# A perceiver layer with a mixture of experts: the router's work moved from behind the attention rounds into them

## The reference, cut to what matters

```
x = x + cross_attention(ctx, layernorm(x))
x = x + linear_attention(layernorm(x))     # 16 heads of 64, elu + 1, causal over 32 tokens, sigmoid gate
xt = layernorm(x)                          # the router and the experts work on this
scores = xt @ gate_w.T                     # 8 experts
top_vals, top_idx = top_k(scores, 2)
top_w = softmax(top_vals)
h = silu(xt @ w1[e].T) * (xt @ w3[e].T)    # 1024 wide
x = x + sum over the two chosen e of top_w * (h @ w2[e].T)
```

## Time and profile before

| | us |
|---|---|
| median of 3 runs | 910.84 (908.56 to 913.74) |
| the profiled execution's own time | 905.29 |
| its span | 903.4 |
| TensorE busy | 811.7 (90%) |
| VectorE busy | 632.5 (70%) |
| ScalarE busy | 540.0 (60%) |
| GpSimd busy | 231.6 (26%) |
| first gather of the expert stage starts at | 508.21 |

### The profile page before, as it was taken

One profiled execution on the slowest core, in us unless ns is written; L12 is line 12 of the kernel. 1 busy time (PEld: TensorE's weight loads), 2 busy tenths in 40 slices (PEclk: granted clock), 3 DMA queues, 4 the chain that ended last, 5 costly groups with the idle time before them and its releaser, 6 DMA issues.

```text
span 903.4 us, 24127 instructions
## 1 busy us (share of the span) xinstructions
PE 811.7 (90%) x9192; PEld 704.3 (78%) x9192; DVE 632.5 (70%) x973; ACT 540.0 (60%) x846; POOL 231.6 (26%) x133
## 2 busy tenths in 40 slices
PE   3889869999999999998582699999999999999994
PEld 2555539889999899896582579888898898888984
DVE  3234332647567475563648399999999999999992
ACT  2433326726445365352131188898999989999881
POOL 1344410000000000000000024554555545555541
PEclk9899999999999999998655599999999999999997
DMA  9799970000000000006372125454554554545542
GB/s 351 274 391 387 382 298 1 3 4 1 3 2 3 4 3 3 3 3 274 112 269 93 58 91 142 122 153 131 139 149 120 153 136 131 152 124 149 142 117 58
DMA packets 34663, 115.84 MB, mean 128 GB/s; under 512 B 4290, under 2 KB 15491, under 8 KB 29475
## 3 DMA queue, kind: packets, MB, share of 16 engines
q1 hardware_dynamic: 27010, 104.35, 33.3%
q0 software_dynamic: 7584, 10.49, 6.5%
HBM read 105.26 MB, written 9.57 MB: 127 GB/s over the span
## 4 chain that ended last, share of the span: by engine, by line
PE 82%; DMA 7%; DVE 6%; issue 2%; ACT 1%; SPq 1%; POOLq 0%; DVEq 0%; ACTq 0%
PE ps L428 21%; PE ps L429 20%; PE ps L430 20%; DMA ctx_t<-in_ctxT 4%; PE ps L734 3%; PE ps L614 3%; PE ps L593 2%; PE ps L602 2%; PE ps L686 2%; PE ps L507 1%; PE ps L671 1%; PE ps L485 1%; PE ps L664 1%; PE ps L697 1%; PE ps L504 1%
## 5 line engine op out<-in xcount | busy, mean ns | idle before, releaser
L403 POOL DMA_INDIRECT xs_sb<-xn_d,slot_row x39 | 68.4, 1753 | 461.6 <-DVE slot_row L1315 384.7
L1195 DVE TENSOR_TENSOR w_lo<-w,w_hi 128x1024 fp32r<-128x1024 f32 x156 | 185.3, 1207 | 0.4 <-issue 0.4
L910 ACT ACTIVATE w_hi<-w 128x1024 fp32r x156 | 161.4, 1064 | 8.4 <-DVE tile_e L1276 7.3
L414 POOL DMA_INDIRECT out_x<-y_sb,slot_row x39 | 120.2, 3082 | 123.0 <-ACT y_sb L942 123.0
L428 PE MATMUL ps<-w_hi,xh 128*128 128x512 f32 x312 | 127.2, 408 | 1.3 <-DVE xl L1338 1.3
L430 PE MATMUL ps<-w_hi,xl 128*128 128x512 f32 x312 | 122.9, 394 | 0.0
L429 PE MATMUL ps<-w_lo,xh 128*128 128x512 f32 x312 | 122.9, 394 | 0.0
L428 PE MATMUL ps<-xT_hi,wa_hi 128*128 128x256 f32 x384 | 112.6, 293 | 1.5 <-DVE xT_lo L1089 1.5
L429 PE MATMUL ps<-xT_lo,wa_hi 128*128 128x256 f32 x384 | 108.9, 284 | 0.0
L430 PE MATMUL ps<-xT_hi,wa_lo 128*128 128x256 f32 x384 | 108.7, 283 | 0.0
L921 ACT ACTIVATE w_hi<-w_sb 128x1024 fp32r<-128x1024 f32 x78 | 82.8, 1062 | 34.1 <-DMA w_sb<-in_w 29.7
(11 more groups left out here) (180 smaller groups left out, 1690.3 us busy)
## 6 DMA issues: line engine op xcount, KB each, us to landing
w_sb<-in_w SPq DMA_DIRECT2D x78, 512.0 KB, 4.7
ctx_t<-in_ctxT SPq DMA_DIRECT2D x16, 1028.0 KB, 7.6
ctx_n<-in_ctxN SPq DMA_DIRECT2D x16, 1024.0 KB
w<-in_w SPq DMA_DIRECT2D x8, 2048.0 KB, 12.0
stage<-in_w_a SPq DMA_DIRECT2D x16, 256.0 KB, 5.4
x_all<-in_x SPq DMA_DIRECT2D x4, 512.0 KB, 7.4
out_x<-x_all SPq DMA_DIRECT2D x1, 2048.0 KB, 13.8
xn_d<-xn SPq DMA_DIRECT2D x4, 512.0 KB, 4.4
```

What stands on the lines that cost most here:

```text
L403: pool.indirect_dma_start(xs_sb[:, :], None, xn_d, bass.IndirectOffsetOnAxis(slot_row[:, t:t + 1], 0)).then_inc(f_xs, 16)
L414: pool.indirect_dma_start(out, bass.IndirectOffsetOnAxis(slot_row[:, t:t + 1], 0), y_sb[:, :], None, compute_op=ALU.add).then_inc(f_st, 16)
L910: act.activation(w_hi[:, c, :].rearrange("p (c n) -> p c n", c=DC), w13[:, bass.ds(e, 1), c % 2, :, c // 2 * 512:(c // 2 + 1) * 512].rearr ...
L1195: dve.tensor_tensor(w_lo[:, c, :].rearrange("p (c n) -> p c n", c=DC), w13[:, bass.ds(e, 1), c % 2, :, c // 2 * 512:(c // 2 + 1) * 512].re ...
```

## The change

The router's work for two tiles is done in the attention rounds, two rounds later: astep(r) does it for round r-2, and the last part for round r-3. There are eleven steps now, astep(0) to astep(10), in place of nine.

Each step has: the row statistics of round r-1 behind x2 (g_stats); the root on ScalarE behind den (g_sqrt), and the row scales on VectorE (g_rstd); the two normed tiles on ScalarE (g_lns); four transposes (g_trs) behind the sixth projection; their eviction (g_xT_ev); four logits products (g_logits) behind the second gate; their copy (g_scores); the two largest and their indices, one-hot choices and running counts (g_top) between the two gated halves; the exponential on ScalarE (g_exp), the weights (g_weights); two rank products (g_ranks) behind the first output projection; the place of each token inside its expert (g_places) with eight comparisons over 128 columns; and twelve scalings on ScalarE (g_whats). In the next step four products of 384 columns (g_table) add the round's tokens to a table by virtual tile, of which each expert has 16, and g_accept adds it up in SBUF. At the end, when all rounds are in, VectorE makes the experts' totals, offsets and a 0/1 selection matrix, and three products take the 39 used tiles out of the 128 virtual ones.

The numerators have three new waits, the second projection one. norm_att is cut in two, the first half placed earlier. The buffers gol and goT lie where expert 0's weights go, so that experts 0, 2 and 3 are loaded when the last projection is done, and only expert 1 early. POOL writes the output's residual and the normed tiles, two transfers a round. The four low splits of the first expert tile on VectorE stand in pairs behind the slot rows and behind the first x_lo.

```
+        load_expert(1)
         sp.wait_ge(a_v, 4 * NT // 2)
         for e in range(E // 2, E):
             load_expert(e)
         sp.wait_ge(a_num, NT)
         sp.wait_ge(a_y, NT // 2)
-        for e in range(EARLY + 1, E // 2):
+        for e in (0, 2, 3):
             load_expert(e)
-
-        sp.wait_ge(a_x2, NT // 2)
...
+        for r in range(NT // 2):
+            rows = slice(2 * r * P, (2 * r + 2) * P)
+            pool.wait_ge(a_x2, r + 1)
+            pool.dma_start(out[rows, :].rearrange("(t p) d -> p t d", p=P), x_all[:, 2 * r:2 * r + 2, :]).then_inc(o_init, 16)
+            pool.wait_ge(g_ln, 2 * r + 2)
+            pool.dma_start(xn_d[rows, :].rearrange("(t p) d -> p t d", p=P), xn3[:, r % 2, :, :]).then_inc(g_keep[r % 2], 16)
...
+                if n == 1:
+                    wait(pe, g_rk, 2 * (r - 2))
...
+            wait(pe, g_xT, r)
+            wait(pe, g_sc, r)
+            wait(pe, g_acc, r - 1)
...
+        def g_trs(r, u):
+            if not valid(r, NR):
+                return
+            wait(pe, g_ln, 2 * r + 2)
+            for dc in range(DC):
+                for s in range(2):
+                    m = pe.transpose(ps[:, 6, dc * 2 * P + s * P:dc * 2 * P + (s + 1) * P],
+                                     xn3[:, u, s, dc * P:(dc + 1) * P], ident)
+            m.then_inc(g_tr, 1)
+        def g_logits(r):
...
+            wait(pe, g_xT, r + 1)
+            wait(pe, a_de, min(2 * r + 4, NT))
+            for s in range(2):
+                for dc in range(DC):
+                    m = pe.matmul(ps[:, 5, s * E:(s + 1) * E], xT3[:, dc, s * P:(s + 1) * P], gw[:, dc, :],
+                                  start=dc == 0, stop=dc == DC - 1)
+            m.then_inc(g_mm, 1)
+        def g_ranks(r):
...
+            wait(pe, g_both, r + 1)
+            wait(pe, a_vu, min(4 * r + 12, 2 * NT))
+            pe.matmul(ps[:, 1, 0:2 * E], con[:, C_LOW:C_LOW + P], both[:, :, :].rearrange("p t e -> p (t e)"), start=True, stop=False)
+            pe.matmul(ps[:, 1, 0:2 * E], ones, count[:, 2 * r:2 * r + 2, :].rearrange("p t e -> p (t e)"),
+                      start=False, stop=True).then_inc(g_rank, 1)
+        def g_table(r):
...
+            wait(pe, g_what, r + 1)
+            wait(pe, a_de, min(2 * r + 6, NT))
+            for n in range(2 * TOP):
+                m = pe.matmul(ps[:, 4, 0:3 * P], in_tile[:, n, :], what[:, n, :, :].rearrange("p k s -> p (k s)"),
+                              start=n == 0, stop=n == 2 * TOP - 1)
+            m.then_inc(g_tab, 1)
             if now:
-                a_qks(r, range(2, 8))
-                a_gates(r)
+                a_qks(r, range(2, 6))
+            g_trs(r - 2, u)
+            if now:
+                a_qks(r, range(6, 8))
+                a_gates(r, range(0, 2))
+            g_logits(r - 2)
+            g_table(r - 3)
+            if now:
+                a_gates(r, range(2, 4))
             for s in range(2):
                 if before:
...
+                if s == 0:
+                    g_ranks(r - 2)
...
+        wait(pe, g_both, NR)
+        pe.matmul(ps[:, 3, 0:E], ones, count[:, NT, :], start=True, stop=True).then_inc(r_sum, 1)
+        pe.wait_ge(g_acc, NR)
+        pe.wait_ge(r_sel, 1)
+        pe.matmul(ps[:, 2, 0:SLOT_TILES], table[:, 0, :], sel[:, :], start=True, stop=True)
+        pe.matmul(ps[:, 2, SLOT_TILES:2 * SLOT_TILES], table[:, 1, :], sel[:, :], start=True, stop=False)
+        pe.matmul(ps[:, 2, SLOT_TILES:2 * SLOT_TILES], table[:, 2, :], sel[:, :], start=False, stop=True).then_inc(r_tab, 1)
...
+        def g_sqrt(r):
...
+            wait(act, g_var, r + 1)
+            act.activation(rstd3[:, :], rstd3[:, :], ACT.Sqrt, bias=eps[:, 0:1]).then_inc(g_sq, 1)
+        def g_lns(r, u):
...
+            wait(act, g_rs, 2 * r + 2)
+            wait(act, g_keep[u], 16 * (r // 2))
+            for s in range(2):
+                act.activation(xn3[:, u, s, :], x_all[:, 2 * r + s, :], ACT.Identity, scale=rstd3[:, s:s + 1],
+                               bias=shift3[:, s:s + 1]).then_inc(g_ln, 1)
+        def g_whats(r):
...
+            wait(act, g_pos, 8 * r + 8)
+            wait(act, g_w, r + 1)
+            wait(act, g_tab, r)
+            for n in range(2 * TOP):
+                t = 2 * r + n // TOP
+                for k, factor in enumerate((con[:, C_ID1 + t:C_ID1 + t + 1], w_h[:, n:n + 1].bitcast(F32), w_l[:, n:n + 1].bitcast(F32))):
+                    m = act.activation(what[:, n, k, :], in_slot[:, n, :], ACT.Identity, scale=factor)
+            m.then_inc(g_what, 1)
+            g_sqrt(r - 2)
             if now:
-                elu_parts(r, range(2, 8))
+                elu_parts(r, range(2, 4))
+            g_lns(r - 2, u)
+            if now:
+                elu_parts(r, range(4, 8))
+            g_xT_ev(r - 2)
+            if now:
                 for n in range(4):
...
+            g_exp(r - 2)
+            g_whats(r - 2)
...
+        def g_rstd(r):
...
+            wait(dve, g_sq, r + 1)
+            dve.reciprocal(rstd3[:, :], rstd3[:, :]).then_inc(g_rs, 1)
+            wait(dve, g_rs, 2 * r + 1)
+            dve.scalar_tensor_tensor(shift3[:, :], mean3[:, :], -0.5, rstd3[:, :], ALU.mult, ALU.mult).then_inc(g_rs, 1)
...
+        def g_top(r):
...
+            wait(dve, g_sc, r + 1)
+            for s in range(2):
+                dve.max(m8[:, s, :], sc[:, s, :]).then_inc(g_max, 1)
+            wait(dve, g_max, 2 * r + 2)
+            for s in range(2):
+                dve.max_index(i8[:, s, :], m8[:, s, :], sc[:, s, :]).then_inc(g_idx, 1)
...
+        def g_places(r):
...
+            wait(dve, g_what, r)
+            for n in range(2 * TOP):
+                dve.tensor_scalar(in_slot[:, n, :], con[:, C_I128:C_I128 + P], inf[:, n:n + 1], None, ALU.is_equal).then_inc(g_pos, 1)
+            wait(dve, g_pp, 7 * r + 7)
+            wait(dve, g_tab, r)
+            for n in range(2 * TOP):
+                dve.tensor_scalar(in_tile[:, n, :], con[:, C_I128:C_I128 + P], vtile[:, n:n + 1], None, ALU.is_equal).then_inc(g_pos, 1)
+            g_rstd(r - 2)
             recip(r - 1, 1)
+            if before:
+                norm_att(r - 1, 0)
...
-                norm_att(r - 1)
+                norm_att(r - 1, 1)
+            g_accept(r - 3)
+            g_scores(r - 2)
             a_lns(r + 1)
             if before:
-                for s in range(2):
-                    gated(r - 1, 1 - u, s)
-                    gated_lo(r - 1, 1 - u, s)
+                gated(r - 1, 1 - u, 0)
+                gated_lo(r - 1, 1 - u, 0)
+            g_top(r - 2)
+            if before:
+                gated(r - 1, 1 - u, 1)
+                gated_lo(r - 1, 1 - u, 1)
             a_lo_ev(r + 1)
             if r == 0:
                 w_out_lows()
+            g_weights(r - 2)
+            g_places(r - 2)
             if before:
                 x2(r - 1)
-                wait(dve, a_x2, r)
-                for s in range(2):
-                    stats_of(2 * (r - 1) + s, 2, a_bn)
-
+                g_stats(r - 1)
+
...
+        dve.wait_ge(r_sum, 1)
...
+        link(dve.reduce_sum(first[:, :], own[:, :, :], AX.X))
...
+        dve.tensor_scalar(sel[:, :], con[:, C_TILE:C_TILE + SLOT_TILES], goal[:, :], real[:, :], ALU.is_equal, ALU.mult).then_inc(r_sel, 1)
-        up_lo(0, range(4), expert(0))
...
+        up_lo(0, range(2), expert(0))
...
         x_lo(0)
+        up_lo(0, range(2, 4), expert(0))
```

More of the change, by code:

```diff
@@ L205, in build @@
-    assert at["late"] <= LATE_AT + EXP_BYTES
-    xT3 = place("xT3", [P, 2, DC, P])
-    IN_SLOTS = 4
-    sc = place("sc", [P, NT, E])
-    m8 = place("m8", [P, NT, 8])
-    i8 = place("i8", [P, NT, 8], U32)
-    i8f = place("i8f", [P, NT, 8])
-    first = place("first", [P, NT, E])
-    second = place("second", [P, NT, E])
-    both = place("both", [P, NT, E])
-    scan = [place(f"scan{i}", [P, NT + 8, E]) for i in range(2)]
-    cmp = place("cmp", [P, E, MAXT])
-    tiles = [place(f"tiles{i}", [P, 4 + E]) for i in range(2)]
@@ new lines, in build @@
+    dif3 = place("dif3", [P, 2])
+    sum3 = place("sum3", [P, 2])
+    sq3 = place("sq3", [P, 2])
+    rstd3 = place("rstd3", [P, 2])
+    shift3 = place("shift3", [P, 2])
+    sc = place("sc", [P, 2, E])
+    m8 = place("m8", [P, 2, 8])
+    i8 = place("i8", [P, 2, 8], U32)
+    pick = place("pick", [P, 2, TOP])
+    chosen = place("chosen", [P, 2 * TOP, E])
+    both = place("both", [P, 2, E])
+    count = place("count", [P, NT + 1, E])
+    dv = place("dv", [P, 2])
+    e1 = place("e1", [P, 2])
@@ new lines, in build @@
+    in_tile = place("in_tile", [P, 2 * TOP, P], F32R)
+    in_slot = place("in_slot", [P, 2 * TOP, P])
+    what = place("what", [P, 2 * TOP, 3, P], F32R)
+    table = place("table", [P, 3, P])
+    tiles = [place(f"tiles{i}", [P, 4 + E]) for i in range(2)]
+    assert at["low"] <= W13_AT, (at, W13_AT)
+    at["low"] = final_at
+    cmp = place("cmp", [P, E, MAXT])
+    own = place("own", [P, 2, E])
+    first = place("first", [P, 2])
```

(40 more changed lines are left out.)

301 lines of the change are left out of this document (153 added, 148 removed).

## The result

The changed kernel takes 917.97 us in the median of its runs (913.03 to 922.06); the kernel before took 908.56 beside it. The ratio is 1.010 with a 95% interval of 1.0061 to 1.0139, so it is slower by 1.0%. I had forecast 912.8 with a range of 901 to 923: the time lies in the range, and in the "slower" case rather than in the likeliest one.

A forecast was written before the change was run, and what follows sets the result against it. TensorE was taken to bound the attention rounds and an unoverlapped chain the tail. Span 903.4 + 23.7 (rounds) - 21.7 (tail) = 905.4 us, so a median of 912.8; likeliest 908 to 915, range 901 to 923.

The forecast's parts named there:

- "slower" case: Whole kernel: slower than before by more than 0.5% (4.6 us can't be told from no change); chance 0.35.
- What bounds the kernel: TensorE fills attention rounds, so work added there counts in full; nothing overlaps in the 84.3 us from last mask to gather.
- The wait: TensorE, at the transposes after the sixth projection, waits 1.9 us a round for ScalarE's normed tiles, behind two table loads.
- Rival 3: Attention rounds: TensorE isn't stalled at the transposes, giving back 11.4 us, 901.4; chance 0.25, shared with half of it plus short tail.
- rival 2: ScalarE: a table switch costs twice its load, in six steps and before the tail's roots; 18 us more, 931; chance 0.04.
- Added to each round: TensorE in attention rounds: router transposes 0.44, logits 0.65, ranks 0.33, table 0.70; together 2.1 us.
- Rounds: Six attention rounds: 5 x (2.1 + 1.9) + 1 x (1.4 + 1.9) = 23.3 us longer; a round 40.3 instead of 36.3.
- rival 1: Attention rounds: each stall drops TensorE's clock; six falls cost 10 us, 923; chance 0.18, counting falls in most rounds.
- Tail: Last mask to first gather of the expert stage: 62.6 us instead of 84.3, 21.7 saved; bounds 58 and 68.
- The sum: Whole kernel's span: 903.4 + 23.7 - 21.7 = 905.4 us; the median comes to 912.8.
- "no change": Whole kernel: median of 908 to 915 us, a difference under 0.5% (4.6 us); chance 0.40.
- Rival 4: Rounds and tail: more waits, VectorE late for masks or instruction fetches; 1 us a round, 2 in the tail, 921; chance 0.13.

The follow-up runs named there:

- a_logits2: Changed kernel with each round's logits computed twice (eight more products of 8 columns a round): 926.8 us, 1.0209 of the kernel before.
- b_pad: Kernel before with nine unused columns of constants, which move every buffer behind them by 32 bytes: 912.64 us, 1.0044 of the kernel before.
- b_xT32: Kernel before with only xT_hi and the buffers placed behind it moved by 32 bytes: 910.44 us, 1.0018 of the kernel before.
- a_pad24: Changed kernel with 24 more unused constant columns, putting xT_hi at 32 of 128 bytes: 915.07 us, 1.0071 of the kernel before.
- the fastest kernel: Changed kernel with the reciprocal root on VectorE and 24 more unused constant columns: 901.64 us, 0.9928 of the kernel before.
- a_trs_late: Changed kernel with the router's four transposes behind the eighth projection instead of the sixth: 921.68 us, 1.0129 of the kernel before.

## Why the prediction was right or wrong

**What bounds the kernel.** Right for the kernel before, and the mechanism held: work put into a round lengthens it (a_logits2: 0.83 us for 0.81), and work taken from the tail shortens the kernel. But the two don't cancel: the rounds gained 27 to 29 us and the tail lost 19. In the changed kernel the round is bound by TensorE and by a wait for ScalarE together.

**Work added to a round: 2.1 forecast, 2.5 measured, from the start of each group to the start of what follows.** Transposes 0.41 (0.44 forecast), logits 0.81 (0.65), table 0.80 (0.70), ranks 0.45 (0.33). I had taken the lowest of the bounds for the logits, by halving a row at half clock; the upper end was right.

**The wait: 1.9 forecast, 1.2 measured, at the forecast place and for the forecast reason.** It is read best in a round without a standstill of another kind behind its first projection, which starts at 248.55:

```profile
248.55 0.39 PE L443 MATMUL ps<-xT_hi,wa_hi 128*128 128x256 f32 x1
...
259.23 1.08 ACT L920 ACTIVATE xn<-x_all,shift,rstd 128x256 f32<-128x256 f32 x2
...
260.36 0.66 PE L656 MATMUL ps<-con,xn 128*128 128x128 f32 x4 [1.21 <-ACT xn L920]
```

The normed tiles are there at +11.8, 0.3 us before the forecast +12.1, since neighbouring instructions on ScalarE overlap (neg 0.20 behind the root's start). And TensorE comes to the transposes at +10.6, 0.4 later than the forecast +10.2, mostly because its products are slower (at +10.4 with 24 more constants). So part of the short wait is luck. Rival 3, no stall, is excluded, and so is rival 2, a switch at twice the load.

**A term that I didn't have: placement.** "Added to each round" counted instructions only. But the nine constants also moved the operands, and the 192 products of 256 columns a round started 0.120 instead of 0.117 us apart: 0.5 us a round. It is shown that the placement does this (b_pad, b_xT32) and costs 0.44% in the kernel before; in the changed kernel 0.1 of it hides behind the wait and 0.4 shows (a_pad24).

**Rounds: +23.3 forecast for six, +29.2 in the first profile, +27.2 in the second.** A full round was to be 4.0 us longer, 40.3. Less standstills the fifth is 4.5 longer, 40.77 against 36.29: 2.5 of work, 1.2 of wait and 0.5 of slower products are 4.2, and 0.3 stays open. The missed terms go one way (work 0.4, placement 0.5) and the wait goes the other (0.7 too long), so that a forecast only 0.5 us short per round is in part luck. The rest is standstills for which the profile shows no releaser, 6.5 us over six rounds of the first profile and 5.7 of the second against 3.6 before, and the first has a fall of the clock too.

**Clock (rival 1).** The six waits of 1.2 us left it at 1.00. One standstill of 1.66 us before 291.19 was followed by the lower level of 1.2 GHz:

```profile
290.00:292.00 2.00, 0.81 (x5) 0.81 (x5) 1.41 (x4) 0.42 (x2) 0.00 (x0) 0.81 0.32 131
292.00:294.00 2.00, 2.00 (x11) 2.00 (x11) 0.00 (x0) 0.27 (x1) 0.00 (x0) 0.50 0.03 8
294.00:296.00 2.00, 2.00 (x13) 1.76 (x13) 0.69 (x1) 1.32 (x3) 0.00 (x0) 0.84 0.00 0
```

The shares make 2 x (0.38 + 1 + 0.32) = 3.4 us at 1.2 GHz, 1.7 lost, and this round took 43.9 us. So the mechanism exists, but none of the waits for ScalarE set it off. Nor does the length of a standstill decide it: those of 1.82 us before 248.37 in this profile and of 2.39 before 163.49 in the fastest kernel's were not followed by a fall, those of 1.82 and 2.17 in a_trs_late and a_pad24 were.

**Tail: 62.6 forecast, 65.6 and 64.9 measured, 84.3 before.** The step that failed is the second half of the numerators: x2 of round 7 came at +34.4 instead of +32.3, behind the standstill of 1.94 us, for which VectorE's second gating waited 1.57. The kernel before has no such standstill in its numerators. ScalarE's next table load then began at +38.1 instead of +35.7, and all that follows is late by 2.4 to 3.0: the end of the top two at +48.8 (46.0), of the comparisons at +52.9 (50.2), of the scalings at +56.6 (53.7). The chain of totals took 3.5 us (forecast 3.6). The expert loads were no matter, as forecast, though they started with x2 and landed at 511.9, +53.7 instead of +48; the map was there 7 us later.

**The sum.** 905.4 was forecast for the span and 920.2 and 917.8 were measured. Of the 12.4 to the second, the rounds are 3.9, the tail 2.3, the start of the kernel 2.7 (residual add at 130.79 against 128.07), the expert stage 2.7 (397.9 us from gather to end against 395.2), and 0.8 is left for the first rounds. Start and expert stage vary as much between the other profiles (the latter from 393.3 to 397.9), so they are not put down to the change. In medians, 917.97 against 912.8, the miss is 5.2 us, about what rounds and tail give (6.2). But 912.8 was counted from a median of 910.84 of the kernel before, and beside the changed one it took 908.56: forecast was 0.2% more, measured 1.0%, and so the time flatters the forecast by 2 us. The forecast of "no change" failed on the placement, on logits, table and ranks taken too cheap, and on the standstills in rounds and tail; only the wait was taken too dear. Rival 4, 1 us more a round and 2 in the tail, gave 921, and comes closest to what was seen (0.65 a round and 2.3 to 3.0), though it named waits and instruction fetches and half of the extra is placement.

**The larger point.** The prediction had the price of the switches right (2.6 us of ScalarE a round) and took them as given. The runs show that they are the difference between a loss of 1.0% and none: with the root on VectorE the change is at 0.9991, and with its buffers well placed too at 0.9928. Whether the kernel before would gain from another placement as well wasn't tried.

## What to carry to other kernels

A function that needs another table is not worth 0.3 us but 2.9 where it stands between exponentials of a critical chain; ten small operations on an engine that is waiting there anyway are the cheaper root. When work is moved under a stage whose bound is full, price it at full length, and look for what it removes from the tail; here 4.5 to 5 us times six rounds stood against 19. And when a change adds buffers or constants, compare the step of the untouched instructions before and after: if it moved, placement is part of the result, and a few unused columns tell how much. Last, take the standstills without a releaser out of a round before comparing it with another kernel's: here they changed by up to 1 us between profiles of the same kernel and hid terms of 0.4 to 0.8 us.

## What the runs showed of the hardware

The step of a 256-column product depends on where its moving operand lies: 0.117 and 0.116 us with xT_hi at 32 of 128 bytes, 0.120 at 64, 0.119 at 96, with the weights at 96 in each. Why, and whether it is the operand's place alone or its distance to another buffer, no run tells. An instruction of ScalarE starts 1.29 to 1.30 us after the table load in front of it began, in each pair shown here, with no added gap. And TensorE has standstills of 0.14 to 3.2 us with nothing to wait for. Their places belong to the program and only their lengths to the execution: all 99 that were counted in the 14 profiles come at the 127th or 128th of each 256 of its matmuls and weight loads (a few records may be missing), and end 1.2 to 1.6 us after a 16 KB transfer of the instruction queue. An edit that adds instructions moves them, as a_logits2 shows; they make up 3 to 7 us of six rounds here.
